# A state-space phase: projected output copied by ScalarE and added by GpSimd, its head reordered, root tables loaded one phase early

## The chip, the cores and the metric
The kernel runs on one core of a Trainium2 chip. The metric is device time in microseconds (us) from start to end of the program. The kernel before takes 2165.59 us, the median of three runs (2164.03 to 2168.28).

## The reference
The input x has 8 sequences of 256 tokens and 128 features. Six blocks are applied one after the other, each on a layer-normalised x and added to x: a feed-forward graph of attention nodes, attention, the same graph again, a mixture of experts, a state-space block, the mixture of experts again. The state-space block, cut to what matters:

```python
xz = einsum('bld,ed->bel', hidden, in_proj_w)          # 2 x 256 channels
out, out_b = branch(xz), branch(xz reversed in time)   # conv of 4 taps, silu, x_proj -> dt, B, C,
    # delta = softplus(dt_proj(dt) + bias); dA = exp(delta * -exp(A_log)); dBu = delta * B * x
    # h = dA * h + dBu over time (16 states); y = (sum of h * C + D * x) * silu(z)
xf = fftn(x); xc = silu(conv5([xf.real, xf.imag]) + bias); x_out = ifftn(xc)
v = abs(x_out * max(silu(z))); out_f = (v - mean(v)) / sqrt(var(v) + 1e-5)
return einsum('bdl,od->blo', out + out_b reversed + out_f, out_proj_w)
```

## The kernel before, in words
x stays in SBUF as `k.x`, 16 tiles of 128 tokens. Each block is a phase of its own: a Block with one instruction stream per engine, semaphores between the streams, and a barrier at its end. Every engine takes its stream in order. A phase starts with `Front`: ScalarE takes a square root of the variances (`root`, L86), VectorE inverts it (L92) and centres the tiles (L101), TensorE transposes them (L110), ScalarE moves them out of PSUM into `k.xT` (L122). A square root needs another function table than Exp or Silu; where the table changes, an ACT_TABLE_LOAD stands before the instruction, under the same line.

The state-space phase is `mamba_phase` (L1363). Its order is written by hand: `mamba_schedule` (L1329) runs ten steps, and in each step three sequences are in work: `f` (being projected), `m` (being scanned, one sequence behind) and `o` (being finished, two behind). In step n, f.b = n, m.b = n - 1, o.b = n - 2. A step has eight slots (UNITS), one per group of four states and direction: slots 0 to 3 forward, 4 to 7 backward.

Per slot of `m`: TensorE spreads B over four banks (`spread`, L1538, `b_bank`), VectorE multiplies (L1825), ScalarE makes the decays (`decay`, L1692, eight activations), VectorE scans (L1832) and multiplies by C (L1837, spread into `c_bank`), GpSimd halves the result twice (L1954, L1957), TensorE sums it into `y_bank` (`total`, L1550).

For `f`, `project` and ScalarE's `front(f, slot)` alternate in the one PSUM bank `w_bank`: slots 0 and 1 the convolutions (L1443, L1642), slots 2 and 4 B, C and dt (L1464, L1647 to L1650), slots 3 and 5 the step sizes (L1471, L1655), slot 7 z (L1450, L1660). ScalarE's `front` for slots 1 to 5 runs one slot later. In slot 6 ScalarE does the softplus of `f` (L1670 to L1676: Abs, Exp, Ln, each 128x1024).

The Fourier branch of `m` is `frequency`: L1483 and L1492 the transforms, L1503 the 5-tap convolution in nine pieces, L1513 in slot 6 and L1522 in slot 7 the two inverse transforms, 16 matmuls each. ScalarE copies between them: L1701 (`yk`), L1705 (`fc`), L1711, L1717 in slot 6, L1722 (squares) in slot 7. `combine` (L1584) makes, once, weights that join the input projection to the first transform; ScalarE copies them (L1730, L1731), and L1483 waits for these copies.

For `o`: VectorE takes the energy (L1842) at the step's start, ScalarE its root (L1734), then the normalisation follows in slots 0 to 3 (L1847 to L1891, with L1750, L1754 and L1758 on ScalarE). In slot 6 (OUT_SLOT) TensorE projects the result into half of `w_bank` (`project_out`, L1575) and VectorE adds it to `k.x` (`add_output`, L1897). In slot 7 VectorE measures mean and variance of the new x (L1904, L1907).

Order that touches the change. On TensorE slot 7 is: total, direct, `project(f, 7)`, spread of C, L1522. `project(f, 7)` waits for the semaphore `x_sb`, which `add_output` of the same step raises. On ScalarE slot 6 is: front(f, 5), decay(m, 7), L1717, softplus(f); slot 7 is: front(f, 7), L1722, decay(f, 0) for the first channel half. The second half of decay 0 opens the next step, ahead of L1734 and L1701.

Of the kernel before, what the change touches and what calls it, by code (L numbers as in the profile page):

```python
# [35 lines left out]
class Kernel:  # L36


    def __init__(self, nc, d, ctx):
        self.nc, self.d, self.ctx, self.sems = nc, d, ctx, {}  # L40
        self.x = self.sb("x", [P, TT, D])
        self.xT = self.sb("xT", [P, TOK])
        self.ident = self.sb("ident", [P, P])
        self.eps = self.sb("eps", [P, 1])
        self.eps6 = self.sb("eps6", [P, 1])
        self.eps2 = self.sb("eps2", [P, 1])
        self.mv = self.sb("mv", [P, TT, 2])
        self.sd = self.sb("sd", [P, TT])
        self.rs = self.sb("rs", [P, TT])

# [3 lines left out]
    def psum(self, name, shape, ctx, dt=F32):  # L54
        return ctx.enter_context(self.nc.psum_tensor(f"ps_{name}", shape, dt))

# [721 lines left out]
def attn_phase(k, a):  # L778
# [3 lines left out]
    with ExitStack() as ctx:  # L782
# [252 lines left out]
        def _(act):  # L1035
# [27 lines left out]
            for step in steps:  # L1063
                f, m = attn_unit(step, 0), attn_unit(step, SOFT_LAG)
                t, o = attn_unit(step, TURN_LAG), attn_unit(step, PROJ_LAG)
                if step == 1:
                    for pair in range(1, B // 2):
                        front.evacuate(act, pair)
                if t:
                    evacuate(t, 0)  # L1070
                    evacuate(t, 1)
                if m:
                    exponent(m, 0)
                    exponent(m, 1)
                if t:
                    evacuate(t, 2)
                    evacuate(t, 3)
                if f:
                    act.wait_ge(s["v_ps"], f.n + 1)
                    if f.n >= VBUFS:  # L1080
                        act.wait_ge(s["cx_ps"], f.n - VBUFS + 1)
                    nc.scalar.activation(v[:, f.n % VBUFS, :, :, :],
                                         vc[:, :, :].rearrange("p a (h e) -> p a h e", h=4), ACT.Copy).then_inc(s["v_sb"], 1)
                if m:
                    exponent(m, 2)
                    exponent(m, 3)
                if t:
                    context(t)

# [8 lines left out]
def moe_phase(k, tag, following=None):  # L1098
# [4 lines left out]
    with ExitStack() as ctx:  # L1103
# [111 lines left out]
        def _(act):  # L1215
# [9 lines left out]
            for step in steps:  # L1225
                f, t = tile(step, 0), tile(step, TURN_E)
                if t is not None:
                    act.wait_ge(s["tp_ps"], t + 1)
                    if t >= 2:
                        act.wait_ge(s["y_ps"], t - 1)  # L1230
                    nc.scalar.activation(hT[:, t % 2, :, :], tp[t % 2][:, :, :], ACT.Copy).then_inc(s["hT_sb"], 1)  # L1231
                if f is not None:
                    act.wait_ge(s["u_sb"], f + 1)
                    nc.scalar.activation(u1[:, f % 2, :], u1[:, f % 2, :], ACT.Silu).then_inc(s["g_sb"], 1)  # L1234
                if step == 1:
                    exponent(1)

# [125 lines left out]
def mamba_phase(k, w):  # L1363
# [6 lines left out]
    with ExitStack() as ctx:  # L1370
# [34 lines left out]
        norm = Front(k, "mb", ctx, [t[:, i:i + 2, :].rearrange("p a n -> p (a n)") for t in (b_bank, c_bank) for i in (0, 2)], ny)  # L1405
# [4 lines left out]
                 "f_ps", "f_sb", "sq2_sb", "v_sb", "vz_sb", "st_sb", "mv_sb", "sd_sb", "rs_sb", "nm_sb", "vn_sb", "yt_sb", "o_ps", "x_sb"]  # L1410
# [18 lines left out]
        def _(pe):  # L1429
            def project(f, slot):  # L1430
# [15 lines left out]
                elif slot == 7:  # L1446
                    pe.wait_ge(s["u_sb"], 2 * f.b + 2)
                    since(pe, "x_sb", f.b - 1)
# [78 lines left out]
            def spread(m, un, which):  # L1527
# [3 lines left out]
                if un == 0 and m.b == 0:  # L1531
                    pe.wait_ge(norm.xT_sb, B // 2)
                    pe.wait_ge(s["sel_sb"], 1)
                if un == 0:
# [29 lines left out]
            def project_out(o, f, m):  # L1564
# [6 lines left out]
                else:  # L1571
                    pe.wait_ge(s["x_sb"], o.b)
# [15 lines left out]
            def step(f, m, o):  # L1588
                if m and m.b == 0:
                    combine()  # L1590
                for slot in range(UNITS):
# [21 lines left out]
                    if f and f.b == 0 and slot == 3:  # L1613
                        for b in range(2, B):
                            norm.turn(pe, b)
                    if m and slot in (1, 6):
# [7 lines left out]
                    if f and slot == UNITS - 1:  # L1624
# [10 lines left out]
        def _(act):  # L1635
            def front(f, slot):
# [7 lines left out]
                elif slot in (2, 4):  # L1644
# [4 lines left out]
                    nc.scalar.activation(bcf[:, :], w_bank[:, 0, :], ACT.Copy).then_inc(s["bcf_sb"], 1)  # L1649
                    nc.scalar.activation(dts[:, :], w_bank[:, 1, :], ACT.Copy).then_inc(s["dts_sb"], 1)  # L1650
# [73 lines left out]
            def step(f, m, o):  # L1724
                if m:
                    decay(m, 0, range(1, DC))
                if m and m.b == 0:
                    front(m, 7)
                    act.wait_ge(s["gw_ps"], 1)
# [5 lines left out]
                for slot in range(UNITS):  # L1735
# [6 lines left out]
                    if m and slot < UNITS - 1:  # L1742
# [31 lines left out]
                    if f and f.b and slot == 6:  # L1774
                        softplus(f, slice(0, 2))
                    if f and f.b and slot == 7:
# [13 lines left out]
        def _(dve):  # L1790
# [103 lines left out]
            def add_output(o):  # L1894
                dve.wait_ge(s["o_ps"], o.b + 1)
                xs = k.x[:, 2 * o.b:2 * o.b + 2, :]
                nc.vector.tensor_tensor(xs, xs, w_bank[:, 0, :].rearrange("p (t e) -> p t e", t=2), ALU.add)\  # L1897
                    .then_inc(s["x_sb"], 1)

# [9 lines left out]
            def step(f, m, o):  # L1909
                if o:  # L1910
                    energy(o)
                for slot in range(UNITS):
# [4 lines left out]
                    if o:  # L1917
# [10 lines left out]
                        elif slot == OUT_SLOT:  # L1928
                            add_output(o)
# [17 lines left out]
        def _(pool):  # L1947
# [10 lines left out]

            def fetch(b):
# [21 lines left out]
            def step(f, m, o):  # L1981
                for un in range(UNITS):
                    if f and un in BC_SLOTS:
                        parts(f, BC_SLOTS.index(un))
                    if m:
# [122 lines left out]
```

## Time and profile before

| | us |
|---|---|
| median of 3 runs | 2165.59 |
| the profiled execution's own time | 2169.39 |
| its span, first to last instruction | 2167.6 |
| mean granted TensorE clock | 0.965 of full |
| PE busy | 2020.1 (93%) |
| DVE busy | 1686.2 (78%) |
| ACT busy | 1374.7 (63%) |
| POOL busy | 1112.7 (51%) |

PE is TensorE, DVE VectorE, ACT ScalarE, POOL GpSimd, SP the engine that issues most transfers. The state-space phase lies between 1377 and 2098 us of the span; it moves next to nothing over DMA. In a timeline, a line is one instruction or several merged (xN): start, time from the first's start to the last's end, engine, line of the kernel, operation, output<-input, and in brackets how long the engine was idle before it and what released it.

### The profile page before, as it was taken

The page shows a single profiled execution, that of the slowest core. Times are in us where ns is not written, and L with a number is a line of the kernel's source. Part 1 is how long each engine was busy: PE and PEld are TensorE (multiplying, and loading weights), DVE is VectorE, ACT ScalarE, POOL GpSimd, SP SyncE. Part 2 cuts the span into 40 slices and gives each one's busy share as a digit, 9 for nine tenths or more (in the row PEclk, how much of TensorE's full clock was granted, in tenths as well). Part 3 has the DMA queues.
Part 4 walks back from the last instruction along what each step waited for, and adds up shares of the span by engine and source line. Part 5 has one row for each costly group of instructions (what it writes and reads, how often), then busy time and mean ns, then how long its engine had stood idle before and what let it go on. Part 6 is the DMA issues. An engine that isn't in the chain of part 4 may idle for free. (4 is left out here: it accounts for less than half of the span.)

```text
span 2167.6 us, 40610 instructions
## 1 busy us (share of the span) xinstructions
PE 2020.1 (93%) x14620; PEld 1506.8 (70%) x14620; DVE 1686.2 (78%) x2918; ACT 1374.7 (63%) x2687; POOL 1112.7 (51%) x1509
## 2 busy tenths in 40 slices
PE   6999999986999995999999988699999999999878
PEld 4677777754887773677777755577877877877745
DVE  5777777765888875777777765499999999999974
ACT  1677777763777773677777653467586685685633
POOL 3555555623767764555555512345736647556423
PEclk8899999997999997999999997899999999999989
DMA  4655566530000003555555515000000000000000
GB/s 133 148 149 147 146 148 149 145 106 1 2 2 2 2 2 78 151 149 146 149 145 150 150 31 200 1 1 1 1 1 1 1 1 0 1 0 1 1 15 20
DMA packets 147750, 144.94 MB, mean 67 GB/s; under 512 B 14048, under 2 KB 106976, under 8 KB 146912
## 3 DMA queue, kind: packets, MB, share of 16 engines
q1 hardware_dynamic: 127968, 132.91, 22.4%
q10 hardware_dynamic: 19584, 9.44, 2.4%
q8 instruction: 118, 1.93, 0.4%
q14 instruction: 80, 0.66, 0.1%
HBM read 94.07 MB, written 38.80 MB: 61 GB/s over the span
## 5 line engine op out<-in xcount | busy, mean ns | idle before, releaser
L606 DVE TENSOR_REDUCE sb_f_mx<-ps_f_s 128x2 f32<-128x512 f32 x768 | 506.4, 686 | 216.5 <-PE ps_f_s L354 215.6
L530 ACT ACTIVATE sb_f_pt<-ps_f_t 128x1024 f32<-128x1024 f32 x384 | 382.1, 1023 | 114.9 <-issue 56.2
L1954 POOL TENSOR_TENSOR sb_mb_h<-sb_mb_h 128x512 f32<-128x512 f32 x128 | 165.0, 1310 | 303.4 <-DVE sb_mb_h L1837 302.3
L354 PE MATMUL ps_f_s<-sb_f_stack 96*128 96x256 bf16 x1536 | 286.5, 279 | 22.1 <-DMA sb_f_stack<-f_scr 14.1
L1832 DVE TENSOR_TENSOR_SCAN sb_mb_h<-sb_mb_da,sb_mb_h 128x1024 f32<-128x1024 f32 x128 | 304.4, 2418 | 2.7 <-ACT sb_mb_da L1692 2.7
L1503 PE MATMUL ps_mb_f<-sb_mb_fc,sb_mb_cw 128*128 128x256 f32 x1280 | 286.8, 381 | 6.7 <-ACT sb_mb_fc L1705 6.6
L1503 PEld LDWEIGHTS ps_mb_f<-sb_mb_fc,sb_mb_cw 128*128 128x128 f32 x1280 | 239.7, 190 | 41.4 <-ACT sb_mb_fc L1705 8.9
L371 PE MATMUL ps_f_t<-sb_f_stack 128*128 128x256 bf16 x1536 | 232.9, 274 | 6.3 <-ACT sb_f_pt L530 3.3
L1692 ACT ACTIVATE sb_mb_da<-sb_mb_dl,sb_mb_an 128x255 f32<-128x255 f32 x512 | 211.0, 496 | 31.3 <-DVE sb_mb_h L1832 30.7
L354 PEld LDWEIGHTS ps_f_s<-sb_f_stack 96*128 96x128 bf16 x1536 | 140.7, 99 | 109.7 <-issue 41.3
L427 PE MATMUL ps_f_a<-sb_f_pt,sb_f_v 128*32 128x256 f32 x3072 | 188.8, 387 | 1.6 <-ACT sb_f_v L579 1.6
L371 PEld LDWEIGHTS ps_f_t<-sb_f_stack 128*128 128x128 bf16 x1536 | 143.6, 97 | 36.1 <-DMA sb_f_stack<-sb_f_mrow 5.8
L1825 DVE TENSOR_TENSOR sb_mb_h<-ps_mb_b,sb_mb_dx 128x1024 f32<-128x1024 f32 x128 | 150.0, 1212 | 10.3 <-PE ps_mb_b L1538 10.3
L1837 DVE TENSOR_TENSOR sb_mb_h<-sb_mb_h,ps_mb_c 128x1024 f32<-128x1024 f32 x128 | 148.6, 1201 | 1.6 <-PE ps_mb_c L1538 1.6
L1016 POOL TENSOR_SCALAR sb_at_pr<-sb_at_pr,sb_at_rinv 128x256 f32<-128x256 f32 x128 | 115.9, 922 | 60.3 <-DVE sb_at_rinv L939 60.3
L711 POOL CAST sb_f_parts<-sb_f_qf 128x512 bf16<-128x512 f32 x96 | 60.5, 630 | 162.8 <-ACT sb_f_qf L557 162.8
L427 PEld LDWEIGHTS ps_f_a<-sb_f_pt,sb_f_v 128*32 128x32 f32 x3072 | 91.6, 111 | 73.8 <-issue 26.0
L694 POOL TENSOR_SCALAR sb_f_nmx<-sb_f_mx 128x16 f32<-128x16 f32 x96 | 36.3, 378 | 196.9 <-DVE sb_f_mx L606 196.9
L1056 ACT ACTIVATE sb_at_pr<-ps_at_sc,sb_at_nmx 128x256 f32<-128x256 f32 x256 | 118.2, 484 | 5.6 <-DVE sb_at_nmx L933 3.5
L1957 POOL TENSOR_TENSOR sb_mb_h<-sb_mb_h 128x256 f32<-128x256 f32 x128 | 118.6, 949 | 0.0
L715 POOL TENSOR_TENSOR sb_f_r<-sb_f_qf,sb_f_parts 128x512 f32<-128x512 f32 x96 | 113.7, 1185 | 7.7
L720 POOL TENSOR_TENSOR sb_f_parts<-sb_f_r,sb_f_parts 128x512 bf16<-128x512 f32 x96 | 111.7, 1164 | 7.7
(252 smaller groups left out, 4132.7 us busy)
## 6 DMA issues: line engine op xcount, KB each, us to landing
f_scr<-sb_f_parts SPq DMA_DIRECT2D x96, 384.0 KB, 2.7
sb_f_stack<-f_scr SPq DMA_DIRECT2D x192, 192.0 KB, 3.0
sb_f_stack<-f_scr SPq DMA_DIRECT2D x192, 128.0 KB, 3.1
sb_f_stack<-f_scr SPq DMA_DIRECT2D x192, 64.0 KB, 3.3
sb_f_stack<-sb_f_mrow ACTq DMA_DIRECT2D x96, 96.0 KB
sb_mb_cw<-in_cw SPq DMA_DIRECT2D x1, 5120.0 KB, 19.4
sb_prep_wn<-in_wn SPq DMA_DIRECT2D x6, 512.0 KB, 7.7
sb_m_w<-in_w SPq DMA_DIRECT2D x6, 256.0 KB, 3.1
```

What stands on the lines that cost most here:

```text
L354: last = nc.tensor.matmul(s_bank[j % 2][:, h, :], stack[0:ROWS, a.n % STACKS, 0, g * GROUP + pair * 2 + h, half * P:(half + 1) * P], stack ...
L371: last = nc.tensor.matmul(t_bank[i % 2][:, h, :], stack[:, e.n % STACKS, 1, g * GROUP + h, half * P:(half + 1) * P], stack[:, e.n % STACKS ...
L427: last = nc.tensor.matmul(act_bank[h * SLOT:(h + 1) * SLOT, g * N:(g + 1) * N], v[:, u.two, half, g * GROUP + h, :], pt[:, u.two, g, half, ...
L530: nc.scalar.activation(pt[:, e.two, g, half, :, :], t_bank[i % 2][:, :, :], ACT.Exp).then_inc(s["pt_sb"], 1)
L606: nc.vector.tensor_reduce(mx[:, a.two, half, head:head + 2], s_bank[j % 2][:, :, :], AX.X, ALU.max)\
L1503: last = nc.tensor.matmul(f_bank[(1 + oc // 2) % 2][:, (oc % 2) * N:(oc % 2 + 1) * N], cw[:, ic, tap, oc * P:(oc + 1) * P], fc[:, ic, tap: ...
L1692: last = nc.scalar.activation(da[:, un % 2, c, i, 1:N], dl[:, m.parity, r, c, 1:N], ACT.Exp, scale=an[:, r, c, n:n + 1])
L1825: nc.vector.tensor_tensor(hb[:, c, :, :], b_bank[:, :, :], dx[:, m.parity, r, c:c + 1, :].broadcast_to([P, SG, N]), ALU.mult)\
L1832: nc.vector.tensor_tensor_scan(flat, da[:, un % 2, c, :, :].rearrange("p i n -> p (i n)"), flat, 0.0, ALU.mult, ALU.add).then_inc(s["scan_ ...
L1837: nc.vector.tensor_tensor(hb[:, c, :, :], hb[:, c, :, :], c_bank[:, :, :], ALU.mult).then_inc(s["hc_sb"], 1)
L1954: nc.gpsimd.tensor_tensor(hb[:, c, 0:2, :], hb[:, c, 0:2, :], hb[:, c, 2:4, :], ALU.add).then_inc(s["half_sb"], 1)
L1957: nc.gpsimd.tensor_tensor(hb[:, c, 0, :], hb[:, c, 0, :], hb[:, c, 1, :], ALU.add).then_inc(s["hs_sb"], 1)
```

## The change
Four edits.

1. Output projection: `add_output` leaves VectorE. In slot 7 ScalarE copies the half of `w_bank` into `dts` (a tile of SBUF that the projection of `f` also uses) and raises the new semaphore `oc_sb`; GpSimd adds `dts` to `k.x` and raises `x_sb`. TensorE's z projection and the last `project_out` now wait for `oc_sb` in place of `x_sb`. ScalarE's next write of `dts` waits for `x_sb`. VectorE's `measure` still waits for `x_sb`.
2. Head: the transposes use other banks, so that `b_bank` is free early; `combine` and the first spread of B run in slot 4 of the first step; the waits of the first spreads are split accordingly. On ScalarE the decays of unit 1 of the first sequence come before the copies of the combined weights.
3. Root tables: a one-element square root at the end of ScalarE's stream in the attention phase and in both mixture-of-experts phases.
4. Nothing changes in `frequency`: the inverse transforms are in one piece before and after.

```diff
+    def root_table(self):
+        self.nc.scalar.activation(self.spare[:, :], self.eps[:, :], ACT.Sqrt)
...
@@ attn_phase and moe_phase, end of ScalarE's stream
+            k.root_table()
@@ mamba_phase
-        norm = Front(k, "mb", ctx, [t[:, i:i + 2, :].rearrange("p a n -> p (a n)") for t in (b_bank, c_bank) for i in (0, 2)], ny)
+        norm = Front(k, "mb", ctx, [t.rearrange("p a n -> p (a n)") for t in (b_bank[:, 0:2, :], c_bank[:, 0:2, :], c_bank[:, 2:4, :], y_bank[:, :, :])], ny)
@@ TensorE, project(f, 7)
                     pe.wait_ge(s["u_sb"], 2 * f.b + 2)
-                    since(pe, "x_sb", f.b - 1)
+                    since(pe, "oc_sb", f.b - 1)
@@ TensorE, spread
                 if un == 0 and m.b == 0:
-                    pe.wait_ge(norm.xT_sb, B // 2)
+                    pe.wait_ge(norm.xT_sb, B // 2 if which else 1)
                     pe.wait_ge(s["sel_sb"], 1)
-                if un == 0:
+                    pe.wait_ge(s["bc_sb"], 1)
+                elif un in (0, SU):
                     pe.wait_ge(s["bc_sb"], 2 * m.b + 2)
@@ TensorE, project_out
                 else:
-                    pe.wait_ge(s["x_sb"], o.b)
+                    pe.wait_ge(s["oc_sb"], o.b)
@@ TensorE, step
-                if m and m.b == 0:
-                    combine()
...
                     if f and f.b == 0 and slot == 3:
+                        pe.wait_ge(s["xc_sb"], 2)
                         for b in range(2, B):
                             norm.turn(pe, b)
+                    if f and f.b == 0 and slot == 4:
+                        combine()
+                        spread(f, 0, 0)
...
-                    if f and slot == UNITS - 1:
+                    if f and f.b and slot == UNITS - 1:
                         spread(f, 0, 0)
@@ ScalarE, front, slots 2 and 4
+                    if r == 0:
+                        since(act, "x_sb", f.b - 2)
                     nc.scalar.activation(dts[:, :], w_bank[:, 1, :], ACT.Copy).then_inc(s["dts_sb"], 1)
@@ ScalarE, step
                 if m and m.b == 0:
                     front(m, 7)
+                    decay(m, 1)
                     act.wait_ge(s["gw_ps"], 1)
...
-                    if m and slot < UNITS - 1:
+                    if m and slot < UNITS - 1 and (m.b or slot):
                         decay(m, slot + 1)
...
                     if f and f.b and slot == 6:
                         softplus(f, slice(0, 2))
+                    if o and slot == 7:
+                        act.wait_ge(s["o_ps"], o.b + 1)
+                        nc.scalar.activation(dts[:, :], w_bank[:, 0, :], ACT.Copy).then_inc(s["oc_sb"], 1)
                     if f and f.b and slot == 7:
                         front(f, 7)
@@ VectorE
-            def add_output(o):
-                dve.wait_ge(s["o_ps"], o.b + 1)
-                xs = k.x[:, 2 * o.b:2 * o.b + 2, :]
-                nc.vector.tensor_tensor(xs, xs, w_bank[:, 0, :].rearrange("p (t e) -> p t e", t=2), ALU.add)\
-                    .then_inc(s["x_sb"], 1)
...
-                        elif slot == OUT_SLOT:
-                            add_output(o)
@@ GpSimd
+            def add_output(o):
+                pool.wait_ge(s["oc_sb"], o.b + 1)
+                xs = k.x[:, 2 * o.b:2 * o.b + 2, :].rearrange("p t e -> p (t e)")
+                nc.gpsimd.tensor_tensor(xs, xs, dts[:, :], ALU.add).then_inc(s["x_sb"], 1)
...
+                    if o and un == OUT_SLOT + 1:
+                        add_output(o)
                     if m:
                         halve(m, un)
```

## Rows read from the trace of the kernel before

**Rows 1.** Waits, VectorE, 1497 to 2005: waiting <- releaser, total us, times, longest
```profile
DVE sb_x L1897 <- PE ps_mb_w L1575: 10.2, 6, 2.2
```

**Rows 2.** Waits, TensorE, the same stretch and columns
```profile
PE ps_mb_f L1492 <- ACT sb_mb_yk L1701: 3.3, 6, 0.9
PE ps_mb_f L1503 <- ACT sb_mb_fc L1705: 2.1, 5, 0.4
PE ps_mb_b L1538 <- DVE sb_mb_h L1825: 0.9, 5, 0.2
```

**Rows 3.** TensorE timeline, one step: start, us, line, operation, [idle before]
```profile
1666.42 1.88 PE L1483 MATMUL ps_mb_f<-sb_mb_fa,sb_mb_ny 128*128 128x512 f32 x4
...
1741.28 1.03 PE L1450 MATMUL ps_mb_w<-sb_mb_xb,sb_mb_win 128*128 128x256 f32 x4
...
1742.58 7.03 PE L1522 MATMUL ps_mb_f<-sb_mb_gi,sb_mb_uk 128*128 128x512 f32 x16
...
1751.19 1.88 PE L1483 MATMUL ps_mb_f<-sb_mb_fa,sb_mb_ny 128*128 128x512 f32 x4
```

**Rows 4.** ScalarE timeline of the same step
```profile
1664.88 1.08 ACT L1722 ACTIVATE sb_mb_uk<-ps_mb_f 128x512 f32<-128x512 f32 x2 [3.71 <-PE ps_mb_f L1522]
...
1667.28 3.30 ACT L1692 ACTIVATE sb_mb_da<-sb_mb_dl,sb_mb_an 128x255 f32<-128x255 f32 x8
...
1672.42 0.58 ACT L1701 ACTIVATE sb_mb_yk<-ps_mb_f 128x512 f32<-128x512 f32 x1
...
1680.02 0.91 ACT L1750 ACTIVATE sb_mb_vv<-sb_mb_vv,sb_mb_zo 128x256 f32<-128x256 f32 x2 [0.26 <-DVE sb_mb_zo L1850]
...
1715.66 0.39 ACT L1650 ACTIVATE sb_mb_dts<-ps_mb_w 128x256 f32<-128x256 f32 x1
...
1742.97 1.06 ACT L1676 ACTIVATE sb_mb_e<-sb_mb_e 128x1024 f32<-128x1024 f32 x1
```

**Rows 5.** VectorE timeline of the same step
```profile
1671.82 4.46 DVE L1832 TENSOR_TENSOR_SCAN sb_mb_h<-sb_mb_da,sb_mb_h 128x1024 f32<-128x1024 f32 x2
...
1739.75 0.42 DVE L1897 TENSOR_TENSOR sb_x<-sb_x,ps_mb_w 128x256 f32<-128x256 f32 x1 [1.59 <-PE ps_mb_w L1575]
```

**Rows 6.** ScalarE timeline, head of the state-space phase
```profile
1377.34 1.28 ACT L86 ACT_TABLE_LOAD   x1 [3.19 <-PEq L59]
...
1410.01 0.60 ACT L1660 ACTIVATE sb_mb_sz<-ps_mb_w 128x512 f32<-128x512 f32 x1
...
1413.42 0.38 ACT L1731 ACTIVATE sb_mb_gm<-ps_mb_f 128x256 f32<-128x256 f32 x1
```

**Rows 7.** TensorE timeline, first sequence's transforms
```profile
1413.85 1.98 PE L1483 MATMUL ps_mb_f<-sb_mb_fa,sb_mb_ny 128*128 128x512 f32 x4 [0.52 <-ACT sb_mb_gm L1731]
...
1428.92 4.58 PE L1503 MATMUL ps_mb_f<-sb_mb_fc,sb_mb_cw 128*128 128x256 f32 x20 [1.85 <-ACT sb_mb_fc L1705]
```

**Rows 8.** VectorE timeline, head of the phase
```profile
1377.52 0.49 DVE L1935 MEMSET sb_mb_xb<- 128x524 f32 x1 [1.02 <-PEq L59]
1378.98 0.25 DVE L92 RECIPROCAL sb_rs<-sb_sd 128x16 f32<-128x16 f32 x1 [0.96 <-ACT sb_sd L86]
...
1410.56 2.35 DVE L1825 TENSOR_TENSOR sb_mb_h<-ps_mb_b,sb_mb_dx 128x1024 f32<-128x1024 f32 x2 [7.56 <-PE ps_mb_b L1538]
```

**Rows 9.** TensorE timeline, last full step
```profile
2011.01 0.94 PE L1538 MATMUL ps_mb_b<-sb_mb_bc,sb_mb_sel 128*128 128x256 bf16 x4 [3.64 <-DVE sb_mb_h L1825]
...
2020.99 6.27 PE L1503 MATMUL ps_mb_f<-sb_mb_fc,sb_mb_cw 128*128 128x256 f32 x20 [2.67 <-ACT sb_mb_fc L1705]
```

**Rows 10.** Stretch 2020 to 2024: busy of PE, PEld, DVE, ACT, POOL; PEclk; DMA
```profile
2020.00:2024.00 4.00, 3.01 (x8) 2.46 (x9) 4.00 (x4) 4.00 (x10) 0.38 (x1) 0.67 0.00 0
```

**Rows 11.** VectorE timeline, tail of the phase
```profile
2096.14 0.42 DVE L1897 TENSOR_TENSOR sb_x<-sb_x,ps_mb_w 128x256 f32<-128x256 f32 x1 [2.16 <-PE ps_mb_w L1575]
```

**Rows 12.** GpSimd timeline, an elementwise operation of 128x256 in the head
```profile
1394.23 0.67 POOL L1971 TENSOR_TENSOR sb_mb_bcr<-sb_mb_bcf,sb_mb_bc 128x256 f32<-128x256 f32 x1 [9.40 <-ACT sb_mb_bcf L1649]
```

**Rows 13.** ScalarE timeline, entry of the second feed-forward phase
```profile
830.97 1.28 ACT L86 ACT_TABLE_LOAD   x1 [3.64 <-PEq L59]
```

More of the change, by code:

```diff
@@ L49, in __init__ @@
         self.rs = self.sb("rs", [P, TT])
+        self.spare = self.sb("spare", [P, 1])
     def sb(self, name, shape, ctx=None, dt=F32):
@@ L1236, in _ @@
                     exponent(1)
+            k.root_table()
         @block.vector
@@ L1409, in mamba_phase @@
                  "b_ps", "c_ps", "da_sb", "dbu_sb", "scan_sb", "hc_sb", "half_sb", "hs_sb", "y_ps", "ym_sb", "dd_sb", "dd_ps",
-                 "f_ps", "f_sb", "sq2_sb", "v_sb", "vz_sb", "st_sb", "mv_sb", "sd_sb", "rs_sb", "nm_sb", "vn_sb", "yt_sb", "o_ps", "x_sb"]
+                 "f_ps", "f_sb", "sq2_sb", "v_sb", "vz_sb", "st_sb", "mv_sb", "sd_sb", "rs_sb", "nm_sb", "vn_sb", "yt_sb", "o_ps", "oc_sb", "x_sb"]
         s = {n: k.sem(f"mb_{n}", ctx) for n in names}
```

## The prediction

> **What bounds the kernel now.** I first listed what every engine waits for in the eight-sequence state-space loop. VectorE, which adds the projected output to the state (L1897), waits for the projection's matmuls six times between 1497 and 2005 us, 10.2 us together [rows 1]. That is what the change removes. Then I asked who else is full. TensorE waits there only for ScalarE's two copies of the transforms, 3.3 and 2.1 us, and for VectorE's first product, 0.9 us [rows 2], 6.3 us of 508. The reader is to see that TensorE, not VectorE, has almost no slack.
>
> The TensorE timeline of one step says the same: the first transform matmuls of a step (L1483) start at 1666.42 and at 1751.19, so a step takes 84.77 us; from 1741.28 to 1751.19 no group shows a pause ahead of it [rows 3]. VectorE does the same step with one pause of 1.59 us before L1897 [rows 5]. Two engines are nearly full; TensorE sets the pace, and VectorE arrives early and waits for it.
>
> Next the ScalarE timeline, since it receives the new copy. It is idle in places, but where the copy is placed matters. In program order the copy stands in slot 7 after the softplus of the next sequence, whose last logarithm runs from 1742.97 to 1744.03 [rows 4]. And TensorE's z projection (L1450), which today waits for VectorE's addition (over at 1740.17 [rows 5]) and starts at 1741.28 [rows 3], will wait for the copy's semaphore `oc_sb`, because both use the same PSUM bank `w_bank`.
>
> **The change part by part.** Sums are against the profiled execution's own time, 2169.4 us (span 2167.6), which is 3.8 above the median of the three runs, 2165.6.
>
> 1. VectorE loses the wait and the addition: 1.59 + 0.42, about 1.9 us per step start to start [rows 5]. On TensorE's path this is worth little. The 0.2 us wait on VectorE's product is followed by a wait for the copy of `yk` [rows 2], which ScalarE reaches by a fixed chain: squares at 1664.88, decays at 1667.28, root, `yk` at 1672.42, over at 1673.00 [rows 4]. That chain starts from TensorE's own last matmuls, so the second wait grows by what the first loses. What VectorE's lead does give is the 0.26 us for which ScalarE waits at 1680.02 for the strengths [rows 4], ahead of the copy that TensorE needs: five times, -1.3 us.
>
> 2. The copy. ScalarE is free at 1744.03, copies 128x256 from PSUM in 0.39 like its sibling at 1715.66 [rows 4], and frees TensorE near 1744.4 instead of 1741.28: a stall of 3.1 us (2.9 if the copy overlaps the logarithm's end, 3.3 with some latency). Queued behind the stalled L1450 on TensorE are the spread of C and the 7.03 us of L1522, and behind L1522 hang ScalarE's squares and VectorE's energy, so the whole next step starts late. The softplus itself waits for L1513 on TensorE, so the stall isn't caught up by either side. The wait exists from f.b = 2 on: six steps (f.b = 2 to 7). Five count in full: 5 x 3.1 = 15.5.
>
> 3. The sixth is followed by the step without `f`, in which VectorE is the bound and TensorE waits 3.64 for it [rows 9]. There only the decays count: they start 2.4 after the squares and end at 1670.58, while the scan that needs them starts at 1671.82 [rows 4, 5]; the slack is 1.24, so 3.1 - 1.24 = 1.9 goes through. No VectorE cover of its own is left, since the scan waits for the decays.
>
> 4. The clock. After a pause TensorE runs slow for a while: after the 2.67 us pause at 2018.3 the same 20 matmuls took 6.27 instead of 4.58 [rows 7, 9], and the granted clock was 0.67 there [rows 10], that is partly at the lower level (1.2 GHz of 2.4). Pauses of 1.85 us cost nothing: the 4.58 is the one behind such a pause [rows 7]. A stall of 3.1 lies beyond the one that cost 1.7, so each may cost 0 to 1.7; the rows don't say that every such pause does it. I take 1.3 each, nearest to the 2.67 row: 6 x 1.3 = 7.8 (ends 0 and 10.2).
>
> 5. GpSimd's addition: 128x256 takes 0.67 with VectorE quiet [rows 12]. In the loop it starts near 1744.5, ahead of GpSimd's halving of the eighth unit, which can't begin before VectorE's last product anyway; VectorE wants the sum only behind that product. Both its scan and its product lie over it: hidden. In the tail nothing hides it. VectorE's 0.42 at 2096.14 [rows 11] becomes copy 0.39, hand-over 0.14, addition 0.67: +0.8. In the last full step VectorE saves the 0.3 of its addition.
>
> 6. Root tables loaded ahead. At the entries of the second feed-forward phase and of the state-space phase a 1.28 us load stands before the root, directly after the barrier [rows 6, 13]. Both move into the phase before, where ScalarE has finished early. The first gives -1.3. In the second, VectorE's memset (to 1378.01) takes over as what the reciprocal at 1378.98 waits for [rows 8], so -0.95. The one added at the end of the last phase runs beside the final stores: 0. The Trainium skill ("ScalarE: Activation LUTs", What ACT_TABLE_LOAD costs) puts a switch at 1.28 plus a drain of 1.38. By the page the two moves would be worth up to 2.8 more. The trace disagrees: the load begins at 1377.34 and the reciprocal behind the root at 1378.98 [rows 6, 8], 1.64 later, which holds load and root but no such drain.
>
> 7. The head. VectorE's first product, now idle 7.56 until 1410.56 [rows 8], can start near 1403, since the combined weights and the first spread move into slot 4, where TensorE pauses anyway. It is then held by the first decays, so its gain is 4. But it leads nowhere, because TensorE is late next. L1483, at 1413.85 behind the copies of the combined weights [rows 7], must now wait until ScalarE has done z (over 1410.61), a table load 1.28, eight decays 3.29, and only then these copies 0.9 [rows 4, 6]: about 1416.0, +2.2. It has then paused since z's matmuls, which ended just before z started at 1410.01 [rows 6], near 6 us, and by rows 7 and 9 pays another 1.7 of slow clock. Against that, the 1.85 us pause before L1503 at 1428.92 [rows 7] disappears, since TensorE is late itself. Net 2.15 + 1.7 - 1.85 = +2.0, less the 0.95 of point 6: +1.05 (ends -0.8 without slow clock, +1.9 if half of that pause stays). From there TensorE paces the loop, so this counts in full.
>
> The inverse transforms (L1513, L1522) are already whole in both kernels; no line of them changes: 0.
>
> Sum: -1.3 (first table) + 1.05 (head with second table) - 1.3 (strengths) + 15.5 + 1.9 (stalls) + 7.8 (clock) + 0.8 - 0.3 (tail) = +24.15. Own time 2193.5; less 3.8, a median near 2189.7 us.
>
> **The rivals.**
> A. The stall comes, the slow clock doesn't: 24.15 - 7.8 = +16.35, 2181.9 us. For it: a pause of 1.85 costs nothing and between two busy stretches 3.1 may still pass. Against it: 2.67 already cost 1.7 [rows 9]. The Trainium skill ("TensorE: Matmul & The Clock Gate", HAM oscillation) sets the harmful pause above the length of this one, and speaks for this rival; the 2.67 us row disagrees with it.
>
> B. Faster: VectorE sets the step, and TensorE's stall is hidden in slack that the trace shows as busy. The place is slot 6 and 7 of six steps; the price paid back is 10.2 + 6 x 0.34 = 12.3 [rows 1, 5], with -0.3 in the last step, -2.25 of tables and +0.8 in the tail: -14.0, so 2151.6 us. It decides if TensorE could start L1522 more than 3 us later without moving L1483. Against it: L1450, L1522 and L1483 follow without a gap [rows 3], and TensorE waits 6.3 us in 508 [rows 2].
>
> C. No change: ScalarE does the copy early, so that only the heads and tails count, or half the stalls are absorbed and meet the gains: 2162 to 2170. Against it: the ScalarE queue is in order and softplus stands ahead of the copy.
>
> D. More than forecast: GpSimd's addition, held up by VectorE's scans, or a late z, delays VectorE's measure and step sizes too. One further us in each of six steps and full clock losses give 2189.7 + 6 + 2.4, near 2198.
>
> **How the numbers follow.** Forecast (stall with slow clock) 0.61, A 0.22, B 0.07, C 0.04, D 0.06. A measurement of this kernel tells about 0.2% from no change, 4.3 us. So faster 0.07, same 0.04, slower 0.89. The range of 8 in 10 must hold the forecast with 0 to 10.2 of clock and A with short stalls (2.9 each, -1.0, and the head at its lower end, -1.85: 2179); it leaves B and C out: 2177 to 2197. Predicted 2189.7.
>
> **What would show it.** Right: TensorE's L1450 waiting some 3 us for ScalarE's new copy, six times; the copy starting right after the logarithm; steps of 88 to 89.5 us between the L1483; granted clock below 1 behind the stalls; VectorE waiting for the seventh spread of B and for the scan's decays. Wrong: steps of 83 us or less, or L1450 without a wait. If steps are near 87.6 at full clock, A holds. If L1483 of the first sequence starts before 1415 (less the 1.3 and 0.95 ahead of it), point 7 is wrong.

## The result, and the profile after

| | before | after |
|---|---|---|
| median, us | 2165.32 (4 runs, 2164.03 to 2168.28) | 2197.3 (4 runs, 2195.29 to 2198.96) |
| ratio | | 1.0149, interval 1.0136 to 1.0161 |
| profiled execution's own time | 2169.39 | 2196.67 |
| its span | 2167.6 | 2194.9 |

The kernel is 32.0 us slower. 2189.7 was predicted, with a range to 2197: right in sign, 7.6 us short, and 0.3 us outside the range. Of all the runs below one (2205.55, of the kernel with the two other orders) was in a slower state of the core, at a clock of 0.92, and is in no ratio.

First TensorE's waits in the state-space phase of the changed kernel (waiting engine, tile and line, releaser, total us, times, longest), over the whole phase. These answer to [rows 2].

```profile
PE ps_mb_w L1457 <- ACT sb_mb_dts L1791: 18.0, 6, 3.0
PE ps_mb_f L1499 <- ACT sb_mb_yk L1713: 8.6, 7, 3.4
PE ps_mb_f L1490 <- ACT sb_mb_gm L1744: 5.9, 1, 5.9
```

The first is the z projection (L1450 before) behind ScalarE's new copy: six waits, 3.0 us each. The third is the head. Of the second, 3.4 lie in the last step, in which VectorE sets the pace, and up to 0.9 in each of the six before it. VectorE now waits in the loop, but no longer for L1897 [rows 1]; the same view for it (the 9.3 is the head):

```profile
DVE sb_mb_h L1841 <- PE ps_mb_b L1546: 20.7, 8, 9.3
DVE sb_mb_vv L1858 <- ACT sb_mb_uk L1734: 14.3, 6, 3.1
DVE sb_mb_h L1848 <- ACT sb_mb_da L1704: 13.2, 7, 3.3
```

TensorE's timeline of the step of [rows 3], in the changed kernel (start, us, line, operation, [idle before it]), and ScalarE's at one of the stalls, against [rows 4]:

```profile
1751.82 2.04 PE L1457 MATMUL ps_mb_w<-sb_mb_xb,sb_mb_win 128*128 128x256 f32 x4 [3.00 <-ACT sb_mb_dts L1791]
1753.66 1.06 PE L1546 MATMUL ps_mb_c<-sb_mb_bc,sb_mb_sel 128*128 128x256 bf16 x4
1754.51 7.32 PE L1529 MATMUL ps_mb_f<-sb_mb_gi,sb_mb_uk 128*128 128x512 f32 x16
```

```profile
1659.75 1.28 ACT L1688 ACT_TABLE_LOAD   x1
1661.04 1.06 ACT L1688 ACTIVATE sb_mb_e<-sb_mb_e 128x1024 f32<-128x1024 f32 x1
1662.01 0.36 ACT L1791 ACTIVATE sb_mb_dts<-ps_mb_w 128x256 f32<-128x256 f32 x1
```

The copy follows the logarithm directly and takes 0.36; TensorE pauses 3.00 for it. Behind the pause four matmuls of 128x256 take 2.04 instead of 1.03 [rows 3] and the spread 1.06 instead of 0.60: about twice as long. Here is the granted clock (columns as in [rows 10]) at another of the six, the one that cost most. It falls before the pause is over, is at its lower level (1.2 GHz of 2.4) right behind it, and is full again some 6.2 us behind its end (a mean of 0.72 over four us). The first line is the pause itself:

```profile
1838.05:1841.05 3.00, 0.00 (x1) 0.03 (x1) 3.00 (x2) 2.89 (x5) 0.07 (x1) 0.89 0.00 0
1841.00:1845.00 4.00, 3.95 (x10) 2.66 (x11) 2.22 (x2) 1.80 (x2) 1.72 (x1) 0.50 0.00 0
1845.00:1849.00 4.00, 4.00 (x8) 1.56 (x7) 3.90 (x8) 0.00 (x0) 3.72 (x3) 0.72 0.00 0
1849.00:1852.60 3.60, 3.60 (x12) 1.57 (x11) 1.52 (x1) 0.05 (x1) 2.11 (x2) 1.00 0.00 0
```

At the other five the clock falls now just before the end of the pause, now up to 1.0 us behind it: the z projection takes from 1.10 to 2.04 there, and the inverse transform (L1529) from 8.34 to 7.32. So the price has to be read from the whole step, not from the first matmuls.

The steps, from one sequence's first transform matmul (L1490) to the next's, were 83.42, 84.39 and 84.76 or 84.77 five times before, and are 84.13, 89.31, 89.31, 89.23, 90.68, 89.31 and 89.32 now. In the two profiled executions the state-space phase, from its first root to the next phase's, is 34.24 us longer:

| part of the phase | before | after | difference |
|---|---|---|---|
| root to first transform | 35.21 | 39.74 | +4.53 |
| first step (no stall in it) | 83.42 | 84.13 | +0.71 |
| six steps | 508.22 | 537.16 | +28.94 |
| last step and tail | 93.31 | 93.37 | +0.06 |

(Before, the phase's table load lies ahead of the root; measured from the end of the barrier, the first transform is at 36.49 before and 39.74 after, +3.25.) The other phases are 6.9 us shorter in sum in these two executions. 1.3 of it is this same load, which counts ahead of the root, and 1.2 the other table load; the remaining 4.4 lie in phases that differ by up to 3 to 4 us among the executions of this study, with the same code.

### The profile page after: what moved, and what is told of

It reads as the page before. It is cut to its first block and busy times, and to the rows that moved or that the text cites. A ratio compares the mean times of both kernels' runs of the same rounds, so it can differ in the third digit from the quotient of the medians.

```text
span 2194.9 us, 40641 instructions
## 1 busy us (share of the span) xinstructions
PE 2027.6 (92%) x14620; PEld 1509.5 (69%) x14620; DVE 1683.6 (77%) x2910; ACT 1380.2 (63%) x2701; POOL 1126.8 (51%) x1517
```

## The experiments

**The copy ahead of the softplus.** The changed kernel, one ScalarE order changed:

```
-  if f and f.b and slot == 6: softplus(f, slice(0, 2))
-  if o and slot == 7:
+  if o and slot == OUT_SLOT:
       act.wait_ge(s["o_ps"], o.b + 1)
       nc.scalar.activation(dts[:, :], w_bank[:, 0, :], ACT.Copy).then_inc(s["oc_sb"], 1)
+  if f and f.b and slot == 6: softplus(f, slice(0, 2))
```

> The changed kernel with ScalarE's copy of the output projection one place earlier: in slot 6, ahead of the softplus. Theory (TensorE paces the loop; the z projection waits 3.0 us for a copy that stands behind the softplus, and the clock falls behind each of these waits): the six waits of the z projection vanish, steps go from 89.3 to about 84.5 us, L1529 takes 7.03 us at full clock, and the time falls by some 28.8 to about 2168.5. Rival 1 (VectorE sets the step once TensorE isn't held): steps of 82.8, about 2158. Rival 2 (the steps grew through GpSimd's addition or its contention with VectorE's scans): steps stay above 88, over 2190.

2166.18 us median of 10 runs, ratio 1.0009 (1.0 to 1.0019). No wait of the z projection for the copy is left in TensorE's list, and six steps take 84.4 each. So some 31 of the 32 us hang on where this one copy stands in ScalarE's order. VectorE's relief, 1.6 us of wait and an addition in each step, brings 84.76 - 84.40 = 0.36 us a step. The rest of it is now VectorE's own wait for TensorE, in this kernel from 1490 to 2000:

```profile
DVE sb_mb_h L1841 <- PE ps_mb_b L1546: 8.9, 6, 1.5
```

**The stall filled, too long.** The changed kernel; six matmuls whose result nobody reads stand ahead of the wait (they wait only until their bank has been read). Each is one instruction here and two records in the trace:

```
+  if f.b > 1:
+      pe.wait_ge(s["f_sb"], FREQ * (f.b - 1) + 5)
+      for i in range(6):
+          nc.tensor.matmul(f_bank[1][:, :], wop[:, 0, :], yk[:, 0, :], start=True, stop=True)
   since(pe, "oc_sb", f.b - 1)
```

> The changed kernel with six extra matmuls of 512 columns (results unused) in TensorE's stream just ahead of the wait for the copy, from the third sequence on. The stall stays, but TensorE works through it. Theory (about 1.7 of the 4.5 us by which each step grew is slow clock after an idle stall): the clock stays at full, L1529 is back at 7.03, steps of about 87.6, the time falls by 6 x 1.7 = 10 to about 2187. Rival (the clock changes nothing that TensorE's waits don't already set): steps stay at 89.3, 2197. If the extra matmuls outlast the stall, steps grow instead; they take 2.6 us against a stall of 3.0.

2196.72 us (1.0152, 1.0136 to 1.0167), steps of 89.55. TensorE's timeline says why, and that the time alone would have misled:

```profile
1659.15 5.31 PE L1458 MATMUL ps_mb_f<-sb_mb_yk,sb_mb_wop 128*128 128x512 f32 x12
1664.30 1.03 PE L1461 MATMUL ps_mb_w<-sb_mb_xb,sb_mb_win 128*128 128x256 f32 x4
1665.16 0.60 PE L1550 MATMUL ps_mb_c<-sb_mb_bc,sb_mb_sel 128*128 128x256 bf16 x4
1665.60 7.03 PE L1533 MATMUL ps_mb_f<-sb_mb_gi,sb_mb_uk 128*128 128x512 f32 x16
```

The six are twelve matmul records and take 5.15 us, not the 2.6 I had taken them for, so they outlast the pause by 2 us. But the z projection behind them takes 1.03 and the inverse 7.03, the durations of full clock. The step is that of the early copy plus the six: 84.40 + 5.15 = 89.55. Two effects of nearly the same size cancelled: some 2 us more of waiting, and no slow clock. The next run therefore has three.

**The stall filled, exactly.** The same with `range(3)`.

> The changed kernel with three matmuls whose result nobody reads (instead of six, which took 5.15 us) between the sixth B spread and the z projection; they should take about 2.6 us and so end inside the 3.0 us wait for ScalarE's copy. Theory (the stall costs its 3.0 us less the slack, and about 1.7 us more per step because the second inverse after it runs at the slower clock): the second inverse takes about 7.0 instead of 7.3 to 7.8, the steps fall from 89.3 to about 87.6, the time by about 10 us to 2187. Rival (the slower clock after a stall is worth nothing, as the steps with six extra matmuls were no shorter): 2197, steps 89.3.

2184.54 us (1.0088, 1.0071 to 1.0105), six steps of 87.57. TensorE's timeline, and three us of the granted clock (columns as above), which is at 1.00 throughout:

```profile
1661.60 2.74 PE L1458 MATMUL ps_mb_f<-sb_mb_yk,sb_mb_wop 128*128 128x512 f32 x6
1664.67 1.13 PE L1461 MATMUL ps_mb_w<-sb_mb_xb,sb_mb_win 128*128 128x256 f32 x4 [0.34 <-ACT sb_mb_dts L1795]
1665.64 0.60 PE L1550 MATMUL ps_mb_c<-sb_mb_bc,sb_mb_sel 128*128 128x256 bf16 x4
1666.07 7.03 PE L1533 MATMUL ps_mb_f<-sb_mb_gi,sb_mb_uk 128*128 128x512 f32 x16
```

```profile
1664.00:1667.00 3.00, 2.66 (x12) 1.62 (x12) 2.63 (x2) 2.50 (x4) 1.74 (x1) 1.00 0.01 3
```

The matmuls end 0.34 before the copy does; nothing useful runs earlier than in the changed kernel, and each step is 1.74 us shorter (89.31 to 87.57). That is the slow clock's price alone. The stall's own price is 87.57 - 84.40 = 3.17.

**A longer stall.** The changed kernel with a one-element square root, and so a table load, ahead of the copy in the six steps:

```
   if o and slot == 7:
+      if f: nc.scalar.activation(waste[:, :], k.eps[:, :], ACT.Sqrt)
       act.wait_ge(s["o_ps"], o.b + 1)
```

> The changed kernel with a square root of one element on ScalarE between the softplus and the copy of the output, in the six steps that have both: its table load (1.28) and itself (about 0.2) put the copy some 1.5 us later. Theory (the copy ends last in each of the six steps): the z projection waits 4.5 instead of 3.0, each step is 1.5 longer, 90.8, and the time 9 us longer, 2206; a longer stall that brings more slow clock adds up to 1 us per step. Rival (something else near the copy holds the step too, so that 1.5 us later costs less): under 3 us more.

2211.64 us (1.0214, 1.0199 to 1.0229), 14.3 more than the changed kernel. The wait is 27.1 us in six, 4.5 each, as meant; the steps grow from 90.53 in the first to 92.11 in the last. In a late one the inverse behind the stall takes 8.62 where it took 7.32 in the timeline above, behind a z projection and a spread that are as slow as there:

```profile
1942.72 2.04 PE L1458 MATMUL ps_mb_w<-sb_mb_xb,sb_mb_win 128*128 128x256 f32 x4 [4.51 <-ACT sb_mb_dts L1794]
1944.55 1.06 PE L1547 MATMUL ps_mb_c<-sb_mb_bc,sb_mb_sel 128*128 128x256 bf16 x4
1945.41 8.62 PE L1530 MATMUL ps_mb_f<-sb_mb_gi,sb_mb_uk 128*128 128x512 f32 x16
```

In the two traces the six steps are 12.6 us longer. If the longer stall goes to the time in full, that is 9 us for 6 x 1.5, and the other 3.6 are slow clock: 0.3 less than in the changed kernel in the first step (90.53 where 89.3 + 1.5 = 90.8 was due), 1.3 more in the last. This run doesn't separate the two. But since over 9 us come of the delay, nothing else near the copy holds the step.

**The output's change alone.** The kernel before, with the output copied by ScalarE and added by GpSimd, and neither tables nor head.

> The kernel before with the first edit alone: output projection copied by ScalarE, added by GpSimd, no new head, no root tables ahead. Theory: steps of 89.3, six stalls of 3 us; 28.9 us more in the six steps, near nothing at the end, so about 2165.3 + 28.9 + 0.5 = 2194.7. Rival (head and output interact, the new head brings the steps out of phase): below 2185.

2194.4 us (1.014, 1.0125 to 1.0155). The same six waits of 3.0, steps 83.42, 90.7, 89.31, 89.31, 89.16, 90.66, 89.32: here two stalls cost more than the others, in the changed kernel one.

**All but the output's change.** The changed kernel with VectorE adding as before.

> The changed kernel with the output projection as before (VectorE adds it from PSUM): new head and root tables alone. Theory: from the root to the first transform 4.5 us more than before, the first step 0.7 more, the two table loads give 1.3 each ahead of a root: 2165.3 + 5.2 - 2.6 = about 2168; L1490 starts behind a pause of near 6 us. Rival (the head is worth what VectorE's 7.6 us pause promised): 2161 or less.

2166.73 us (1.001, 1.0 to 1.0019): head and tables together cost some 2 us, if anything. The steps are 83.64, 84.41 and 84.77 again. With the run before, 30.0 and 2.4 us more than the kernel before, the two halves of the change add up to 32.4; 32.0 was measured for both together.

**The gating weights' copies first.** In the changed kernel, `decay(m, 1)` of the first sequence goes behind the two copies:

```
-  decay(m, 1)
   act.wait_ge(s["gw_ps"], 1)
   nc.scalar.activation(gw[:, 0:2, :]...)
   nc.scalar.activation(gw[:, 2, :]...)
+  decay(m, 1)
```

> The changed kernel with ScalarE's two copies of the first sequence's gating weights put ahead of the second decay of that sequence instead of behind it. Theory (the first forward transform waits 5.91 us for those copies, 2.2 of it for the decay, and then runs at the slower clock for some 3 us): it starts about 2 to 3 us earlier, the time falls by 3 to 4 us, to 2193 to 2194. Rival (the late start comes from the centring at the phase's entry and the copies are not last): no change. Second rival (VectorE, which reached the seventh B spread with 9.3 us to wait, is not bound by the transform): no change in the end, though the transform starts earlier.

2191.15 us (1.0118, 1.0103 to 1.0133), 6.1 less, where 3 to 4 were expected. TensorE at the first transform, in the changed kernel and in this one:

```profile
1411.43 3.78 PE L1490 MATMUL ps_mb_f<-sb_mb_fa,sb_mb_ny 128*128 128x512 f32 x4 [5.91 <-ACT sb_mb_gm L1744]
```

```profile
1405.50 1.98 PE L1490 MATMUL ps_mb_f<-sb_mb_fa,sb_mb_ny 128*128 128x512 f32 x4 [1.32 <-ACT sb_mb_gm L1743]
```

A wait of 1.32 in place of 5.91, and full clock behind it: root to first transform 34.11 instead of 39.74, first step 81.30 instead of 84.13. Of the 5.63 between 39.74 and 34.11, 4.59 are the shorter wait; 1.05 is the phase's very first convolution (5.67 here, 6.72 in the profiled execution of the change), which the order doesn't touch. So the changed head is behind the old one only because of this order; with the two lines exchanged it is 2.4 us ahead from the barrier on (34.11 against 36.49) and 2.1 in the first step.

**GpSimd held back at the phase's entry.** The changed kernel with one wait:

```
   pool.wait_ge(w.loaded, LOADS)
+  pool.wait_ge(norm.y_sb, 1)
```

> The changed kernel in which GpSimd waits for the end of the first half of the centring of the state-space phase before it starts its first multiplication of wc. Theory (the root table loaded early gives nothing there because GpSimd's multiplication, 2.34, then lies beside VectorE's 16 subtractions, 7.78 instead of 6.68 before): the subtractions take 6.7 again and everything behind them starts 1.1 earlier, time about 1 us shorter, 2195 to 2196, unless the late multiplication becomes the wait of the first product. Rival (the multiplication is what the first product of the phase waits for): up to 2.3 us longer, 2199.

2195.55 us (1.0141, 1.0126 to 1.0156), not to be told from the changed kernel. My expectation of the centring was wrong: it takes 8.56, longer still. `y_sb` counts pairs of tiles, so this wait is over after two of the 16 subtractions, not after half of them, and GpSimd's multiplication falls among the others. The busy time of the subtractions (L106) in three stretches of this kernel (stretch, length, busy us, count, clock, DMA share, GB/s), the middle one that in which GpSimd multiplies, and in the changed kernel in two, the first ending with GpSimd's multiplication:

```profile
1374.10:1374.88 0.78, 0.75 (x3) 0.88 0.00 0
1374.88:1377.22 2.34, 2.34 (x2) 0.50 0.00 0
1377.22:1382.70 5.48, 5.47 (x13) 0.50 0.01 3
```

```profile
1372.49:1374.03 1.54, 1.54 (x1) 0.60 0.00 0
1374.03:1380.30 6.27, 6.24 (x16) 0.50 0.01 3
```

(An instruction across a border counts in both.) All 16 in this kernel, with the shortest, median and longest in ns:

```profile
L106 DVE TENSOR_SCALAR sb_mb_ny<-sb_x,sb_mv,sb_rs x16: 334/336/2439, 1374.1 to 1382.4; 128x128 f32<-128x128 f32 x16
```

While GpSimd multiplies for 2.34 us, VectorE ends the subtraction that it is in; the next takes 2.44 instead of 0.34. The wait moved the standstill, it didn't take it away. The kernel before has such a standstill too, later: GpSimd's second multiplication (1382.43, 2.40 us) lies over one of its subtractions, the longest of which is 2.44. The changed kernel has that one and most of another at the start, this one has two whole ones: 6.68, 7.78 and 8.56 of centring. A wait for the end of the whole centring was not tried.

**The two roots alone**, in the kernel before.

> The kernel before with the two one-element roots at the ends of phases and nothing else. Theory: the table load of 1.28 leaves the entry of the second fold phase (1.28 shorter) and gives nothing at the entry of the state-space phase, whose centring stretches from 6.7 to 7.8 beside GpSimd: 2163.2, ratio 0.9994. Rival (both entries gain): 2162.0. Rival (neither does, the load only moves): 2164.5.

2165.4 us median of 12 runs beside 2164.32 of 24 of the kernel before (1.0001, 0.9992 to 1.001). No gain can be told; the interval would still hold one of 1.3.

**The two other orders, output as before.** The changed kernel with VectorE adding, the weights' copies first, and `frequency(m, 0)` and `frequency(m, 1)` (the copies of yk and fc) ahead of the square root and of the scaling by zo.

> The changed kernel with the output added to the state by VectorE as before, and with the two orders on ScalarE of the faster kernel that have nothing to do with the output: the gating weights ahead of the second decay, the copies of yk ahead of the square root. Theory (with the 0.86 us wait of the second product's operand gone VectorE sets the step, and its wait for the output and its addition come back on the path): the steps are 84.4 to 84.8 instead of 84.07, the time 2158 to 2161. Rival (the wait and the addition are hidden still): 2155.6, the same as with the output copied by ScalarE; then the moved output is worth nothing in any order.

2159.01 us (0.9974, 0.9965 to 0.9983), steps of 84.42.

**All three orders, output as in the change.** The copy of the output early, the weights' copies first, and:

```
+  if m: frequency(m, 0)
   if o:
       act.wait_ge(s["sq2_sb"], o.b + 1)
       nc.scalar.activation(vv[:, :, :], vv[:, :, :], ACT.Sqrt)
   ...
-  if m and slot <= 1: frequency(m, slot)
   ...
+  if m and slot == 0 and m.b: frequency(m, 1)
   if o and slot == 0:  # vv times zo
```

> The changed kernel with three orders on ScalarE changed: the copy of the output in the slot ahead of the softplus; the gating weights' copies ahead of the second decay of the first sequence; the copies of yk ahead of the square root and of the scaling by zo. Theory: the six stalls of 3.0 go (as in the kernel with the copy early, 2166.2), the head gives 3 us, and the wait of the second inverse's operand, 0.86 in each of six steps, goes, steps 83.6: about 2158. Rival (VectorE is behind TensorE by less than 0.9 us a step and takes over): 2162.

2155.59 us median of 5 runs (0.9961, 0.9948 to 0.9974): the fastest, 9 us ahead of the kernel before and 41.7 ahead of the change. Its steps are 83.59 once, then 83.88 and 84.03 to 84.08, not 83.6 throughout: VectorE took over, as the rival had it, though the time is below both expectations (2158 and 2162). One step of it, busy time of PE, PEld, DVE, ACT and POOL, then the clock:

```profile
1739.46:1823.54 84.08, 83.48 (x387) 64.87 (x386) 83.56 (x66) 58.72 (x113) 52.39 (x43) 1.00 0.00 1
```

Both engines are over 99% busy. The moved addition is worth 84.42 - 84.07 = 0.35 a step by the traces; whether the two totals differ stays open, since their intervals overlap.

**The same with GpSimd's wait at the entry.**

> The kernel with the three orders on ScalarE changed (2155.6) and GpSimd's wait for the first half of the centring. Theory: the entry of the state-space phase gives 1 us, 2154.5. Rival: the delayed product costs what the centring gives, 2155.6 to 2157.

2158.99 us (0.9975, 0.9965 to 0.9985), no better, and above what was expected either way; the first convolution starts 5.99 us after the root instead of 5.22, since VectorE's third subtraction now stands still, ahead of the second pair of transposes that the convolution waits for.

## Why the prediction was right and wrong, step by step

Right was the mechanism: an in-order queue on ScalarE, a shared bank, six stalls of 3.0 (3.1 foreseen), steps of 88 to 89.5 (89.3, once 90.7), VectorE late behind TensorE, a new wait for the decays. Rivals B and C fall with the six waits and with the run that has the copy early; A, at 2181.9, with the exact filling, which removes what A denies and gives 2184.5. D's 2198 is near the time measured, but by half of its cause only: the clock losses in full, yes; GpSimd's addition delaying VectorE in each step, no (it did so once, see part 5).

Part 1, VectorE's relief, 0.26 a step: 0.36 measured, and ScalarE's wait for the strengths (1.3 in five before) is gone from its list with the copy early. Right.

Part 2, the stall, 3.1: 3.17. Right.

Part 3, the sixth stall, 1.24 absorbed: the last step's first scan stood 5.38 behind the transform before and 4.18 after, so 1.2 was absorbed. But the last step and tail together came out at +0.06 instead of some -0.7. In the tail, copy and GpSimd's addition cost 0.76 (VectorE's last L1891 or L1907 to its measure: 3.31 and 4.07; 0.8 foreseen). What was missed is the last pair of scans before the tail. It takes 4.64 in the kernel before and 5.45 in the changed one, in which GpSimd's addition lies beside it:

```profile
2078.78 4.64 DVE L1832 TENSOR_TENSOR_SCAN sb_mb_h<-sb_mb_da,sb_mb_h 128x1024 f32<-128x1024 f32 x2
```

```profile
2104.49 5.45 DVE L1848 TENSOR_TENSOR_SCAN sb_mb_h<-sb_mb_da,sb_mb_h 128x1024 f32<-128x1024 f32 x2
2105.07 2.73 POOL L1971 TENSOR_TENSOR sb_x<-sb_x,sb_mb_dts 128x256 f32<-128x256 f32 x1
```

The two halves of the change tell which it is, all but the output's change first, the output's change alone second:

```profile
2075.95 4.64 DVE L1843 TENSOR_TENSOR_SCAN sb_mb_h<-sb_mb_da,sb_mb_h 128x1024 f32<-128x1024 f32 x2
```

```profile
2101.49 5.45 DVE L1837 TENSOR_TENSOR_SCAN sb_mb_h<-sb_mb_da,sb_mb_h 128x1024 f32<-128x1024 f32 x2
```

Part 4, the clock, is the step of the prediction that failed most, by its size: "I take 1.3 each". The exact filling shows 1.74 a step, and one stall of the six cost 1.4 more (step 90.68; its inverse 8.78), so 6 x 1.74 + 1.4 = 11.8 in the place of 7.8, beyond even the end of 10.2. I had a row that cost 1.7 behind a pause of 2.67 [rows 9] and marked it down because the rows didn't say that every such pause does it. All six did. The six steps add up: -6 x 0.3 of relief, +6 x 3.17, +11.8 is +29.0, and 28.94 was measured. What made one stall dearer is not shown. The Trainium skill ("TensorE: Matmul & The Clock Gate", HAM oscillation) puts the harmful idle gap above the length of these; the profile, with six of six pauses of 3.00 us followed by the lower clock, disagrees.

Part 5, GpSimd's addition hidden in the loop: right, nobody waits for it there. But "both its scan and its product lie over it: hidden" fails in the last full step, in which VectorE sets the pace: there the scans beside the addition take 0.81 longer, and instead of saving 0.3 VectorE loses 0.5.

Part 6: at the second feed-forward phase, from VectorE's last aggregate to the first transpose 4.11 before and 2.88 after, so the 1.3 came. At the state-space phase the 0.95 did not: the first transposes start 2.74 behind the barrier in both. What the reciprocal waits for did change (it starts 0.57 behind the barrier instead of 1.62), but the first subtraction then stands still until GpSimd's multiplication is over, 2.34 behind the barrier. Compare these with [rows 8]:

```profile
1371.85 0.49 DVE L1943 MEMSET sb_mb_xb<- 128x524 f32 x1 [1.02 <-PEq L64]
1372.26 0.20 DVE L97 RECIPROCAL sb_rs<-sb_sd 128x16 f32<-128x16 f32 x1
1372.49 7.78 DVE L106 TENSOR_SCALAR sb_mb_ny<-sb_x,sb_mv,sb_rs 128x128 f32<-128x128 f32 x16
```

```profile
1371.69 2.34 POOL L2008 TENSOR_TENSOR sb_mb_wc<-sb_mb_wc,sb_mb_win 128x1024 f32<-128x1024 f32 x1 [4.64 <-SPq L1377]
```

Before, the load had covered that; its removal uncovered it. The 0.95 foreseen for this entry is a term of the prediction that was put down without looking at GpSimd. The Trainium skill ("SBUF — State Buffer", SBUF: two separate sides) says that an operation of GpSimd and some of VectorE's exclude each other for the whole instruction; the subtraction of 2.44 us beside a multiplication of 2.34 agrees.

Part 7, the head: the copies behind the second decay, +2.15, came: z starts at 1402.59 and the transform at 1411.43, 8.84 apart where before it was 6.68 (1407.17 to 1413.85). The slow clock behind the pause of 5.91 cost 2.87, not 1.7 (L1490 3.78 for 1.98, the convolution after it 4.69 for 3.62). The phase's very first convolution took 6.72 and not 5.63, +1.1; it took 5.17 to 6.72 in the kernels of this study, so this belongs to the execution. Foreseen for head and tables was +1.05 with the 0.95 in it, measured from the barrier +3.25 + 0.71 = +3.96: 0.95 of the table, 1.2 of slow clock and 1.1 of the first convolution are 3.2, 0.3 more than the gap of 2.9. That L1483 (L1490 now) would not start before 1415 less 2.25 can be read only relative to the barrier, which itself should come 1.3 earlier: that is 36.7 behind it; it came at 39.74.

So of the 7.6 us missed in the median, 4.0 are the clock behind the six stalls, about 2.9 the head, and 0.8 the last pair of scans, each read in one execution of either kernel. The agreement with the median is partly luck: the phases around this one differ by some us from execution to execution.

## What to carry to other kernels

A copy that hands a PSUM bank back belongs into the slot in which its data are ready, ahead of any long chain in the same queue: here one place in ScalarE's order was worth 31 us, while the engine that was relieved gave 2. Ask of each moved operation not what it costs but what stands ahead of it and who waits behind it; and when TensorE is the one who waits, count its slow clock with the stall, in full, where one row already shows it. An order that gives 0.3 a step is worth looking for only when the engine that it speeds up sets the step, and then the next engine is close behind: here each order gave 0.3 to 0.4 a step (84.77 to 84.40 to 84.07) before the other engine held it.

## What the runs showed of the hardware

Pauses of 3.00 us on TensorE were followed by the lower of its two clocks six times out of six in the changed kernel, at 1.7 us each (3.1 once), where a pause of 1.85 had cost nothing [rows 7]. In the three other runs with the same six pauses (output alone, weights first, GpSimd held back) the steps are 89.0 to 90.7 against 87.57 at full clock, so none of the 24 pauses was free: 19 cost 1.4 to 1.8, five 3.0 to 3.1. With pauses of 4.5 the steps were 90.5 to 92.1 where 89.3 + 1.5 = 90.8 was due. Three f32 matmuls of 128x512, recorded as six, kept the clock up through the pause at no cost, the only case here in which useless work paid: 12.8 us.

Beside GpSimd's f32 multiplication of 128x1024 (2.34 to 2.40 us) one of VectorE's f32 subtractions of 128x128 took 2.44 us instead of 0.34, in the kernel before, in the changed one and with the multiplication held back.

VectorE's scan pair of 128x1024 took 4.46 to 5.40 in one step of the kernel before, and about the same in the same place in the others. The last pair of the phase took 4.64 in all kernels in which VectorE adds the output and 5.45 in those in which GpSimd adds it, beside that pair; GpSimd's addition of 128x256 then took 2.7 us there, 0.72 in the tail with VectorE waiting. What sets the other differences no run here isolates.
